# Projecting the first chunks before the attention jobs, or between them

## The chip, the cores and the metric

The kernel runs on one core of a Trainium2 chip. The metric is the device time of one execution in microseconds (us), the median of several runs. Times inside an execution are read from a profile of one such execution and count from its first instruction.

## What is computed

Two transformer layers on `x` of 4 sequences x 1024 rows x 128 columns, in fp32. Each layer adds attention (16 heads of 8 columns) and then a gated feed-forward net, each on the layer-normalised `x`. The attention of the first layer sees all keys, that of the second is causal. The core of the reference:

```python
def attention(x, Wqkv, bqkv, Wout, bout):
    qkv = (x @ Wqkv + bqkv).reshape(b, s, H, 3 * HD)
    q, k, v = qkv[..., :HD], qkv[..., HD:2 * HD], qkv[..., 2 * HD:]
    scores = jnp.einsum('bqhd,bkhd->bhqk', q, k) / jnp.sqrt(HD)
    out = jnp.einsum('bhqk,bkhd->bqhd', jax.nn.softmax(scores), v)
    return out.reshape(b, s, e) @ Wout + bout

x = x + attention_a(layernorm(x));  x = x + ffn(layernorm(x))
x = x + attention_b(layernorm(x));  x = x + ffn(layernorm(x))
```

The weights of the net are integers that are scaled by 1/127 first.

## The kernel before, in words

**Tiling.** The 4096 rows are 8 chunks of 512 (`CHUNKS`), two to a sequence. For each chunk VectorE computes the row statistics (`row_moments`), POOL raises the variance to the power -0.5 (`inverse_deviation`), VectorE normalises four tiles (`normalise`, line 706), TensorE transposes them (`transpose_tiles`, line 938), ScalarE copies the result (`copy_xt`), and TensorE makes the products (`qkv_products`: q and k at line 948, v at line 950). ScalarE takes q and k with their bias and rounds them (`take_qk`, lines 528 and 532); VectorE adds the bias to v and writes it into the tile `v`, and then subtracts the rounded q and k from the exact ones (`split_chunk`, lines 725 and 729), so that a q or k is held as two parts. The SyncE queue (SP) writes the parts to DRAM (`store_parts`).

**Windows.** Attention runs over 16 windows: one sequence and 4 of its heads each. SP loads the queries and keys of a window from DRAM into one of three buffers of `qop` and `kop` (`load_operands`, 14 DMAs). Rows of `qop` and `kop` that no load writes must be filled once with zeros and ones. TensorE's *jobs* (line 995) compute scores for their row maxima alone, 64 for a window in layer one, and VectorE reduces each to a maximum (`run_job`, line 785, or 782 on the diagonal). Jobs use a ring of three PSUM banks. When a half of a window (512 queries) has its 32 jobs, VectorE negates the maxima (`negate_max`), POOL splits them (`split_shift`), TensorE transposes them, ScalarE copies them to `shift_rows`, and SP writes them by two DMAs into the last rows of `qop` (`shift_to_operand`, line 373). Only then can TensorE compute the shifted *scores* of that half (line 1009), whose exponential ScalarE takes (line 559) and which TensorE multiplies with v (line 1045).

**Order.** The engines each run a hand-made list. `Plan` makes it. `plan.before` is what comes ahead of the steady part in each layer: in layer one 54 jobs, with the shift of the first half after job 35 and scores from job 42 on. The *turns* follow, one for each window: the scores of window w between the rest of its jobs and the first jobs of window w + 1. Between the two layers there is a `middle` part, in which the feed-forward net of layer one runs and the chunks are projected for layer two.

**Start of layer one before.** VectorE runs the moments and the normalising of chunks 0 and 1, statistics of chunks 2 to 7 at once, then all eight chunks in one pipeline (`first_chunk` on each engine), then the scaling of the integer weights (line 767). POOL fills `v` with ones between the power of chunk 0 and that of chunk 1 (line 437), and the rows of all three `kop` buffers after the latter (line 444). ScalarE fills the rows of all three `qop` buffers first (line 510). SP's queue in order: stores of chunks 0 to 3, loads of window 0, stores of chunks 4 to 7, loads of window 1, the first shift. TensorE starts with jobs when `qk_ready` and `v_ready` say that all eight chunks are taken; after jobs 4, 8 and 12 it transposes a third of the scaled weights (line 971).

## Time and profile before

| what | us |
|---|---|
| median of 3 runs | 1576.52 |
| lowest and highest | 1567.07, 1581.94 |
| the profiled execution's own time | 1573.21 |
| its span, first to last instruction | 1571.4 |
| TensorE, VectorE, ScalarE busy in it | 1438.6, 1235.9, 980.0 |

### The profile page before, as it was taken

How to read it: one execution, taken by the hardware profiler on the slowest of the kernel's cores; microseconds unless marked ns; L12 is line 12 of the kernel's file. 1: busy time of each engine (PE TensorE's matmuls, PEld its weight loads, DVE VectorE, ACT ScalarE, POOL GpSimd, SP SyncE). 2: the span in 40 equal slices, each digit the busy share in tenths (PEclk: the TensorE clock that was granted, in tenths of full speed). 3: DMA queues.
4: the chain of work that ended last, by engine and by line, in shares of the span. 5: the costliest groups of instructions: out<-in, count | busy, mean ns of one | idle time of the engine just before them, and what ended most of it. 6: DMA issues, size and time to landing. Idle time of an engine off the chain costs nothing.

```text
span 1571.4 us, 26128 instructions
## 1 busy us (share of the span) xinstructions
PE 1438.6 (92%) x9625; PEld 701.7 (45%) x9625; DVE 1235.9 (79%) x3106; ACT 980.0 (62%) x1259; POOL 108.9 (7%) x210
## 2 busy tenths in 40 slices
PE   3699999999999999999988988999999999999888
PEld 2444344434444443444436654444444444444455
DVE  7589999999999998999937757787787877777254
ACT  4427777777777777777774432666666666666622
POOL 6020000000000000000001112000000000000010
PEclk9859999999999999999999985999999999999999
DMA  3720111111101111110001323111121112210000
GB/s 95 221 57 7 27 28 29 29 29 28 28 6 25 28 28 29 28 28 2 2 1 54 83 79 76 35 29 29 29 53 32 29 29 47 38 29 2 8 21 27
DMA packets 40055, 58.39 MB, mean 37 GB/s; under 512 B 7796, under 2 KB 19448, under 8 KB 39928
## 3 DMA queue, kind: packets, MB, share of 16 engines
q1 hardware_dynamic: 39928, 56.72, 15.2%
q8 instruction: 76, 1.25, 0.3%
q14 instruction: 51, 0.42, 0.1%
HBM read 36.77 MB, written 18.87 MB: 35 GB/s over the span
## 4 chain that ended last, share of the span: by engine, by line
PE 70%; DVE 18%; ACT 5%; issue 4%; DMA 2%; SPq 1%; POOL 0%; DVEq 0%; ACTq 0%; POOLq 0%
PE psum L995 25%; PE psum L1045 23%; DVE maxima L785 11%; PE psum L1009 6%; PE psum L1142 5%; PE psum L938 4%; ACT probs L559 3%; DVE junk L782 3%; PE psum L1147 2%; PE psum L1017 1%; PE psum L948 1%; DVE xn L706 1%; PE psum L1062 1%; DMA k_parts<-parts 1%; DMA qop<-shift_rows 1%
## 5 line engine op out<-in xcount | busy, mean ns | idle before, releaser
L559 ACT ACTIVATE probs<-psum 128x1024 f32<-128x1024 f32 (+3 forms) x896 | 794.2, 932 | 300.4 <-PE psum L1009 192.7
L785 DVE TENSOR_REDUCE maxima<-psum 128x1 f32<-128x512 f32 x1280 | 815.2, 684 | 72.8 <-PE psum L995 67.8
L995 PE MATMUL psum<-kop,qop 62*128 62x512 f32 (+3 forms) x1792 | 657.0, 465 | 56.5 <-DVE maxima L782 20.0
L1009 PE MATMUL psum<-qop,kop 64*128 64x512 f32 (+3 forms) x1792 | 498.2, 411 | 10.4 <-ACT probs L559 7.8
L995 PEld LDWEIGHTS psum<-kop,qop 62*128 62x128 f32 x1792 | 289.6, 191 | 487.6 <-DVE maxima L785 325.4
L1045 PE MATMUL psum<-probs,vwin 128*32 128x512 f32 (+3 forms) x3584 | 441.6, 565 | 3.9 <-ACT probs L559 2.0
L782 DVE CUSTOM_DVE_ANT_0 junk<-psum,mask 128x384 bf16<-128x384 f32 (+3 forms) x512 | 237.4, 487 | 75.3 <-PE psum L995 69.8
L1009 PEld LDWEIGHTS psum<-qop,kop 64*128 64x128 f32 x1792 | 242.0, 189 | 55.7 <-ACT probs L559 44.7
L1045 PEld LDWEIGHTS psum<-probs,vwin 128*32 128x32 f32 x3584 | 71.8, 109 | 105.5 <-issue 84.6
L1017 PE MATMUL psum<-half_ident,key_mask 64*128 64x64 bf16 x1024 | 92.7, 198 | 0.0
L1142 PE MATMUL psum<-ffn_xt,wffn 128*128 128x512 f32 x192 | 87.6, 594 | 0.0
L463 POOL TENSOR_TENSOR shift<-negmax,zeros 128x16 bf16<-128x16 f32 x64 | 14.1, 220 | 1017.5 <-DVE negmax L791 1017.5
L796 DVE RECIPROCAL rden<-att_raw 128x16 f32<-128x16 f32 x64 | 15.8, 247 | 61.3 <-ACT att_raw L580 61.3
L656 ACT ACTIVATE hid<-psum 128x512 f32<-128x512 f32 x48 | 28.7, 597 | 52.0 <-PE psum L1142 52.0
L1147 PE MATMUL psum<-wffn,hid 128*128 128x128 f32 x384 | 48.7, 278 | 7.9 <-DVE hid L899 7.9
L1017 PEld LDWEIGHTS psum<-half_ident,key_mask 64*128 64x128 bf16 x1024 | 49.7, 97 | 13.1 <-issue 1.3
L899 DVE TENSOR_TENSOR hid<-psum,hid 128x512 f32<-128x512 f32 x48 | 32.4, 689 | 26.8 <-PE psum L1142 21.4
L1147 PEld LDWEIGHTS psum<-wffn,hid 128*128 128x128 f32 x384 | 45.2, 192 | 15.4 <-DVE hid L899 15.4
L575 ACT CAST shift_rows<-psum 32x128 f32<-32x128 bf16 x64 | 16.3, 254 | 56.7 <-PE psum L1027 56.7
L714 DVE TENSOR_TENSOR x<-psum,x 128x512 f32<-128x512 f32 x32 | 22.1, 690 | 37.4 <-PE psum L1147 29.1
L1142 PEld LDWEIGHTS psum<-ffn_xt,wffn 128*128 128x128 f32 x192 | 34.2, 191 | 31.9 <-issue 31.0
L938 PEld LDWEIGHTS psum<-ident,sums 128*128 128x128 f32 x256 | 26.8, 140 | 44.9 <-ACT probs L559 40.2
(88 smaller groups left out, 709.9 us busy)
## 6 DMA issues: line engine op xcount, KB each, us to landing
qop<-q_parts SPq DMA_DIRECT2D x256, 64.0 KB
q_parts<-parts SPq DMA_DIRECT2D x32, 256.0 KB, 3.0
k_parts<-parts SPq DMA_DIRECT2D x32, 256.0 KB, 3.4
kop<-k_parts SPq DMA_DIRECT2D x64, 128.0 KB
kop<-k_parts SPq DMA_DIRECT2D x128, 64.0 KB
x<-in_L_attn_a_x SPq DMA_DIRECT2D x8, 256.0 KB, 4.4
qop<-shift_rows SPq DMA_DIRECT2D x128, 8.0 KB
out_x<-x SPq DMA_DIRECT2D x8, 256.0 KB, 2.3
```

The lines of the kernel that those rows point to most:

```text
L559: nc.scalar.activation(probs[:, slot, :, c0:], psum[:, bank:bank + 2, c0:], ACT.Exp, scale=SCORE_SCALE).then_inc(probs_ready, 1)
L656: nc.scalar.activation(hid[:, c, :], psum[:, 2 + 2 * (c % 2), :], ACT.Silu).then_inc(silu_ready, 1)
L782: nc.vector.tensor_tensor_reduce(out=junk[:, slot, 0:width], in0=src, in1=mask[:, CHUNK - width:], scale=1.0, scalar=LOWEST, op0=ALU.add, ...
L785: nc.vector.tensor_reduce(dst, src, AX_X, ALU.max).then_inc(ring_free, 1)
L899: nc.vector.tensor_tensor(hid[:, c, :], psum[:, 3 + 2 * (c % 2), :], hid[:, c, :], ALU.mult).then_inc(hid_ready, 1)
L938: ins = nc.tensor.transpose(psum[:, bank, t * P:(t + 1) * P], src[:, t, :], ident[:])
L995: mm(psum[:, slot, 0:width], qop[rows, buf, f, r, qb * P:(qb + 1) * P].bitcast(F32R), kop[rows, buf, r, kh * CHUNK:kh * CHUNK + width].bit ...
L1009: ins = mm(psum[:, bank + h, c0:], kop[rows, buf, pair, j * P:(j + 1) * P].bitcast(F32R), qop[rows, buf, f, pair, c0:].bitcast(F32R), star ...
L1017: ins = mm(psum[:, bank + h, at:at + TILE_ROWS], key_mask[rows, part, :], half_ident[rows], start=False, stop=part == 1)
L1045: ins = mm(psum[32 * c:32 * c + 32, 7, c0:], vwin[:, buf, at:at + 32], probs[:, slot, c % 2, c0:], start=(j == 0), stop=(s == plan.half_en ...
L1142: mm(psum[:, 2 + 2 * (c % 2) + k, :], wffn[:, k, c, :], ffn_xt[:], start=True, stop=True).then_inc(gate_up_psum, 1)
L1147: ins = mm(psum[:, 7, t * P:(t + 1) * P], hid[:, c, t * P:(t + 1) * P], wffn[:, 2, c, :], start=(c == 0), stop=(c == FB - 1))
```

## The change

- The list of layer one gets new events: before jobs 4, 9, 14, 19, 24 and 29 a chunk (2 to 7), before job 34 the weights. Ahead of the jobs only chunks 0 and 1, the first sequence, are projected. At event n each engine does: VectorE normalises chunk n + 1 and splits chunk n - 1; TensorE transposes chunk n + 1 and multiplies chunk n; ScalarE copies and takes them. In the jobs' part v has one PSUM bank and q and k have two, since the ring takes the others. The weights event also splits chunk 7.
- SP stores chunks 0 and 1, then loads window 0, then stores chunks 2 to 7, then loads window 1. `load_operands` waits itself for the stores of its sequence alone. It takes the keys and first queries first and counts the four DMAs of the second half's queries on another semaphore. Each chunk of `x` has a semaphore of its own, and the weights of layer two are loaded after `x`.
- POOL fills a quarter of `v` with its first constants, the rest after chunk 1 is normalised, and the `kop` rows of buffers 1 and 2 after the last chunk is normalised. ScalarE fills the rows of `qop` and `kop` for buffer 0 first, those of `qop` buffers 1 and 2 in the chunk events 2 and 3.
- The statistics of chunks 2 to 7 come in three pieces while VectorE would wait. The biases of layer two are spread after the products of chunk 1.

The core of the diff (blank lines left out):

```diff
+        chunk_at = {4 + chunk_jobs * i: ("chunk", 2 + i) for i in range(CHUNKS - 2)} if chunk_jobs else {}
+        weights_at = 4 + chunk_jobs * (CHUNKS - 2)
...
+            if k in chunk_at:
+                events.append(chunk_at[k])
+            if chunk_jobs and k == weights_at:
+                events.append(("weights",))
...
-    LOADS = 2 * 7 * SEM_DMA
+    LOADS = 2 * 5 * SEM_DMA
+    LATE_LOADS = 2 * 2 * SEM_DMA
...
             load_x(0, x_loaded[0])
-            for l, (w, b, bo) in enumerate(((wqkv_a, bqkv_a, bout_a), (wqkv_b, bqkv_b, bout_b))):
-                sp.dma_start(wqkv_raw[:, l, :], w).then_inc(qkv_weights_loaded, SEM_DMA)
-                sp.dma_start(bias_raw[0:1, l, :], b.rearrange("(o n) -> o n", o=1)).then_inc(qkv_weights_loaded, SEM_DMA)
-                sp.dma_start(bias_row[0:1, l, 3, :], bo.rearrange("(o n) -> o n", o=1)).then_inc(qkv_weights_loaded, SEM_DMA)
-            load_x(1, x_loaded[1])
-            for c in range(2, CHUNKS):
-                load_x(c, x_loaded[2])
+            load_qkv_weights(0, wqkv_a, bqkv_a, bout_a)
+            for c in range(1, CHUNKS):
+                load_x(c, x_loaded[c])
+            load_qkv_weights(1, wqkv_b, bqkv_b, bout_b)
...
-            def load_operands(w, buf):
+            def load_operands(layer, w, buf):
                 q_heads = q_parts[bass.ds(w, 1)].rearrange("o (r i) d t -> i d (o r) t", i=2)
                 k_heads = k_parts[bass.ds(w, 1)].rearrange("o (r i) d t -> i d (o r) t", i=2)
+                def load_queries(i, f, loaded):
+                    for row in (TILE_ROWS * i, TILE_ROWS * i + PD):
+                        sp.dma_start(qop[row:row + PD, buf, f], q_heads[i, :, :, f * CHUNK:(f + 1) * CHUNK]).then_inc(loaded, SEM_DMA)
+                for p in range(2):
+                    sp.wait_ge(parts_stored[p], (layer * B + w // GROUPS + 1) * STORES)
                 for i in range(2):
                     base = TILE_ROWS * i
-                    for f in range(2):
-                        for row in (base, base + PD):
-                            sp.dma_start(qop[row:row + PD, buf, f],
-                                         q_heads[i, :, :, f * CHUNK:(f + 1) * CHUNK]).then_inc(operands_loaded[buf], SEM_DMA)
+                    load_queries(i, 0, operands_loaded[buf])
                     for row, part in ((base, slice(0, PD)), (base + PD, slice(HD, PD)), (base + PD + HD, slice(0, HD))):
                         sp.dma_start(kop[row:row + part.stop - part.start, buf], k_heads[i, part]).then_inc(operands_loaded[buf], SEM_DMA)
+                for i in range(2):
+                    load_queries(i, 1, late_operands_loaded[buf])
             for layer, plan in enumerate(PLANS):
-                for i in range(B // 2):
+                for half in range(2):
+                    store_parts(layer, 0, half)
+                if layer == 0:
+                    load_operands(layer, 0, 0)
+                for i in range(1, B):
                     for half in range(2):
                         store_parts(layer, i, half)
-                for p in range(2):
-                    sp.wait_ge(parts_stored[p], (layer * B + B // 2) * STORES)
-                if layer == 0:
-                    sp.wait_ge(ones_ready, 2)
-                    sp.wait_ge(operands_zeroed, 2)
-                load_operands(0, 0)
-                for i in range(B // 2, B):
-                    for half in range(2):
-                        store_parts(layer, i, half)
-                for p in range(2):
-                    sp.wait_ge(parts_stored[p], (layer + 1) * B * STORES)
-                load_operands(1, 1)
+                    if layer == 1 and i == 1:
+                        load_operands(layer, 0, 0)
+                load_operands(layer, 1, 1)
...
+            nc.gpsimd.memset(v[:, 0:GROUPS * VW], 1.0).then_inc(v_set, 1)
...
-            nc.gpsimd.memset(v[:], 1.0).then_inc(v_set, 1)
             inverse_deviation(2, first_moments[:, :, TPC:2 * TPC], 2)
-            pool.wait_ge(rstd_ready[2], 2)
-            for i in range(2):
-                row = TILE_ROWS * i + GUARD_ROW
-                nc.gpsimd.memset(kop[row:row + SCORE_ROWS - GUARD_ROW], 1.0).then_inc(ones_ready, 1)
-                pool.wait_ge(ones_ready, i + 1)
+            pool.wait_ge(xn_ready[0], 2)
+            nc.gpsimd.memset(v[:, GROUPS * VW:], 1.0).then_inc(v_set, 1)
             inverse_deviation(2, first_moments[:, :, 2 * TPC:], 3)
             for layer, plan in enumerate(PLANS):
-                pool.wait_ge(v_ready, (layer + 1) * CHUNKS)
                 sums_base = layer * WINDOWS * PLANS[0].n
                 half_base = layer * 2 * WINDOWS
                 def copy_v(w, buf):
+                    chunks = min(2 * (w // GROUPS) + 2 + (w % GROUPS == GROUPS - 1), CHUNKS)
+                    pool.wait_ge(v_ready, layer * CHUNKS + chunks)
...
+                if layer == 0:
+                    pool.wait_ge(vwin_ready, 2)
+                    pool.wait_ge(xn_ready[0], CHUNKS)
+                    for u in range(1, BUFS):
+                        for i in range(2):
+                            row = TILE_ROWS * i + GUARD_ROW
+                            nc.gpsimd.memset(kop[row:row + SCORE_ROWS - GUARD_ROW, u], 1.0).then_inc(ones_ready, 1)
+                            pool.wait_ge(ones_ready, 2 * u + i - 1)
...
-            for i in range(2):
-                rows = slice(TILE_ROWS * i + GUARD_ROW, TILE_ROWS * i + SCORE_ROWS)
-                nc.scalar.copy(qop[rows].rearrange("p u f r t -> p (u f r t)").bitcast(F32R),
-                               zeros[rows, 0:1].broadcast_to([SCORE_ROWS - GUARD_ROW, BUFS * PAIRS * S])).then_inc(operands_zeroed, 1)
...
+            def fill_rows(tile, u, source):
+                for i in range(2):
+                    rows = slice(TILE_ROWS * i + GUARD_ROW, TILE_ROWS * i + SCORE_ROWS)
+                    dst = tile[rows, u].bitcast(F32R)
+                    nc.scalar.copy(dst, source[rows].broadcast_to([SCORE_ROWS - GUARD_ROW, PAIRS * S])).then_inc(operands_zeroed, 1)
+            qop_rows = qop[:].rearrange("p u f r t -> p u (f r t)")
+            kop_rows = kop[:].rearrange("p u r t -> p u (r t)")
+            fill_rows(qop_rows, 0, zeros[:, 0:1])
+            fill_rows(kop_rows, 0, one[:])
+            def take_biases(l, qk_bank, vo_bank, column):
+                act.wait_ge(setup_psum, l + 1)
+                nc.scalar.copy(bqk[:, l, :], psum[:, qk_bank, 0:2])
+                nc.scalar.copy(bvo[:, l].rearrange("p t e -> p (t e)"), psum[:, vo_bank, column:column + 2 * E]).then_inc(setup_ready, 1)
+            take_biases(0, 6, 7, 0)
...
+            copy_xt(1, 1, 1)
+            take_qk(0, 0, 0, 2)
+            take_qk(0, 1, 1, 5)
+            take_biases(1, 0, 0, 2 * E)
+            copy_xt(2, 0, 0)
+            def chunk(n):
+                if n + 1 < CHUNKS:
+                    copy_xt(n + 1, (n + 1) % 2, (n + 1) % 2)
+                take_qk(0, n, n % 2, 2)
+                if 2 <= n < BUFS + 1:
+                    fill_rows(qop_rows, n - 1, zeros[:, 0:1])
...
+                    if kind == "chunk":
+                        chunk(what[0])
+                    elif kind == "weights":
+                        for k in range(3):
+                            act.wait_ge(setup_psum, 3 + k)
+                            nc.scalar.copy(wffn[:, k].rearrange("p c d -> p (c d)"), psum[:, k, 0:HIDDEN]).then_inc(setup_ready, 1)
...
-            dve.wait_ge(x_loaded[0], SEM_DMA)
-            first_row_moments(0, 1, 0)
-            dve.wait_ge(qkv_weights_loaded, 6 * SEM_DMA)
+                moments_of(2, first_stats[:, tiles], first_moments[:, :, tiles], count)
+            def first_normalise(n):
+                normalise(0, n, first_moments, n * TPC, xn[:, n % 2], n - 1)
+            first_row_stats(0, 1).then_inc(moment_steps[2], 1)
+            first_moments_of(0, 1, 0)
+            dve.wait_ge(qkv_weights_loaded[0], 3 * SEM_DMA)
             order_columns(0)
             dve.wait_ge(rstd_ready[2], 1)
-            normalise(0, 0, first_moments, 0, xn[:, 0], 0)
-            order_columns(1)
-            dve.wait_ge(x_loaded[1], SEM_DMA)
-            first_row_moments(1, 1, 1)
+            first_normalise(0)
+            first_row_stats(1, 1).then_inc(moment_steps[2], 1)
+            first_moments_of(1, 1, 1)
+            first_row_stats(2, 2)
             dve.wait_ge(rstd_ready[2], 2)
-            normalise(0, 1, first_moments, TPC, xn[:, 1], 0)
-            dve.wait_ge(x_loaded[2], (CHUNKS - 2) * SEM_DMA)
-            first_row_moments(2, CHUNKS - 2, 2)
-            dve.wait_ge(rstd_ready[2], 3)
+            first_normalise(1)
+            first_row_stats(4, 2)
             dve.wait_ge(setup_ready, 1)
             dve.wait_ge(v_set, 1)
-            def first_chunk(n, buf, m):
-                if m + 2 < CHUNKS:
-                    normalise(0, n + 2, first_moments, (n + 2) * TPC, xn[:, buf], n + 1)
-                split_chunk(0, n, buf, 4 + 3 * buf)
-            pipeline(dve, first_chunk)
-            dve.wait_ge(other_weights_loaded, 5 * SEM_DMA)
-            nc.vector.tensor_scalar(wflt, wint, DEQUANT, None, ALU.mult).then_inc(wflt_ready, 1)
+            split_chunk(0, 0, 0, 4)
+            first_row_stats(6, 2).then_inc(moment_steps[2], 1)
+            first_moments_of(2, CHUNKS - 2, 2)
+            split_chunk(0, 1, 1, 7)
+            dve.wait_ge(qkv_weights_loaded[1], 3 * SEM_DMA)
+            order_columns(1)
+            dve.wait_ge(rstd_ready[2], 3)
+            first_normalise(2)
+            dve.wait_ge(v_set, 2)
+            def chunk(n):
+                if n + 1 < CHUNKS:
+                    first_normalise(n + 1)
+                if n > 2:
+                    split_chunk(0, n - 1, (n - 1) % 2, 7)
...
+                    elif kind == "weights":
+                        chunk(CHUNKS)
+                        dve.wait_ge(other_weights_loaded, 5 * SEM_DMA)
+                        nc.vector.tensor_scalar(wflt, wint, DEQUANT, None, ALU.mult).then_inc(wflt_ready, 1)
...
+            transpose_xn(1, 1, 1)
             pe.wait_ge(setup_ready, 1)
-            pipeline(pe, first_chunk)
+            qkv_products(0, 0, 0, 2, 4)
+            qkv_products(0, 1, 1, 5, 7)
+            spread_biases(1, 0, 0, 2 * E)
+            pe.wait_ge(setup_ready, 2)
+            transpose_xn(2, 0, 0)
+            def chunk(n):
+                if n + 1 < CHUNKS:
+                    pe.wait_ge(xt_ready[0], n)
+                    transpose_xn(n + 1, (n + 1) % 2, (n + 1) % 2)
+                pe.wait_ge(qk_ready, 2 * n)
+                pe.wait_ge(v_ready, n)
+                qkv_products(0, n, n % 2, 2, 7)
...
+                        if layer == 0 and lap == 0:
+                            pe.wait_ge(operands_zeroed, 4 + 2 * buf)
+                            wait(pe, ones_ready, 2 * buf)
+                    if (f, c, qb, kh) == (1, 0, 0, 0):
+                        earlier = layer * len(range(buf, WINDOWS, BUFS))
+                        pe.wait_ge(late_operands_loaded[buf], (lap + earlier + 1) * LATE_LOADS)
...
-                        if layer == 0 and index in (4, 8, 12):
-                            pe.wait_ge(wflt_ready, 1)
-                            transpose_weights(index // 4 - 1)
+                        continue
+                    if kind == "chunk":
+                        chunk(what[0])
+                        continue
+                    if kind == "weights":
+                        pe.wait_ge(wflt_ready, 1)
+                        pe.wait_ge(xt_ready[0], CHUNKS)
+                        pe.wait_ge(qk_ready, 2 * CHUNKS)
+                        for k in range(3):
+                            transpose_weights(k)
                         continue
                     if layer == 0 and unit == 0:
-                        pe.wait_ge(setup_ready, 4)
+                        pe.wait_ge(setup_ready, 5)
+                        pe.wait_ge(v_ready, CHUNKS)
```

## Rows read from the trace of the kernel before

**Rows 1.** The page: the chain that ended last, share of the span by engine.
```profile
PE 70%; DVE 18%; ACT 5%; issue 4%; DMA 2%; SPq 1%; POOL 0%; DVEq 0%; ACTq 0%; POOLq 0%
```

**Rows 2.** Timeline to 36 us: start, duration (us), engine, line, operation, tiles, shapes, count, [idle before].
```profile
6.49 3.96 POOL L437 MEMSET v<- 128x4631 f32 x1
6.57 4.53 DVE L706 TENSOR_SCALAR xn<-x,first_moments 128x128 f32<-128x128 f32 x4 [0.23 <-POOL first_moments L434]
...
14.81 10.69 DVE L706 TENSOR_SCALAR xn<-x,first_moments 128x128 f32<-128x128 f32 x4 [1.13 <-POOL first_moments L434]
14.83 10.51 POOL L444 MEMSET kop<- 32x6144 f32 x2
...
25.42 4.72 DVE L687 BATCH_NORM_STATS2 first_stats<-x 128x6 f32<-128x128 f32 x24
...
31.34 4.16 POOL L434 TENSOR_TENSOR first_moments<-first_moments,power 128x24 f32<-128x24 f32 x1 [5.99 <-DVE first_moments L700]
```

**Rows 3.** The same timeline: chunks in the projection stretch, at both clock levels.
```profile
26.52 3.11 PE L948 MATMUL psum<-xt,wqkv 128*128 128x512 f32 x4
...
29.47 1.05 PE L950 MATMUL psum<-wqkv,xt 128*128 128x128 f32 x8
...
35.53 1.12 DVE L706 TENSOR_SCALAR xn<-x,first_moments 128x128 f32<-128x128 f32 x4 [4.35 <-POOL first_moments L434]
36.57 0.88 DVE L725 TENSOR_TENSOR v<-psum,bvo 128x128 f32<-128x128 f32 x4
...
36.80 1.09 PE L938 MATMUL psum<-ident,xn 128*128 128x128 f32 x4 [6.28 <-DVE xn L706]
...
37.68 3.62 PE L948 MATMUL psum<-xt,wqkv 128*128 128x512 f32 x4
...
41.09 1.80 PE L950 MATMUL psum<-wqkv,xt 128*128 128x128 f32 x8
...
43.16 1.88 PE L948 MATMUL psum<-xt,wqkv 128*128 128x512 f32 x4
```

**Rows 4.** The same timeline: the first jobs, the weights, the first scores.
```profile
73.41 1.19 PE L995 MATMUL psum<-kop,qop 62*128 62x512 f32 x3 [11.63 <-DVE v L725]
...
75.20 0.75 DVE L767 TENSOR_SCALAR probs<-probs 128x1152 f32<-128x1152 int32 x1
...
80.44 0.90 PE L971 MATMUL psum<-ident,probs 128*128 128x128 f32 x3
...
85.24 12.65 DVE L785 TENSOR_REDUCE maxima<-psum 128x1 f32<-128x512 f32 x21 [0.65 <-PE psum L995]
...
102.28 1.21 PE L1009 MATMUL psum<-qop,kop 64*128 64x512 f32 x2
```

**Rows 5.** Windows: busy us (instructions) per engine, granted clock, DMA share, GB/s.
```profile
90.00:100.00 10.00, 10.00 (x19) 4.83 (x18) 10.00 (x19) 0.26 (x1) 1.86 (x3) 0.50 0.00 1
...
1106.00:1110.00 4.00, 4.00 (x43) 2.11 (x38) 3.48 (x18) 2.15 (x3) 0.00 (x0) 0.70 0.44 118
```

**Rows 6.** Two source lines: the subtraction from 70 to 80 us, POOL's copy; durations ns min/median/max.
```profile
L729 DVE TENSOR_TENSOR parts<-qk,parts x2: 1226/1350/1475, 71.3 to 73.8; 128x1024 f32<-128x1024 f32 x2
...
L454 POOL COPY vwin<-v x32: 439/443/1370, 73.4 to 1391.7; 128x311 f32<-128x311 f32 x32
```

**Rows 7.** The chain in order of time, start of layer two: start, duration (us), what.
```profile
945.66 3.01 DMA k_parts<-parts
...
955.29 4.84 DMA qop<-shift_rows
```

**Rows 8.** Timeline of SP's queue: window 1's loads and the first shift.
```profile
80.30 1.71 SPq L342 DMA_DIRECT2D qop<-q_parts  x4
82.07 1.12 SPq L345 DMA_DIRECT2D kop<-k_parts  x3
...
99.30 1.41 SPq L373 DMA_DIRECT2D qop<-shift_rows  x2
```

**Rows 9.** Timeline of TensorE, first scores of layer two.
```profile
960.18 0.80 PE L1009 MATMUL psum<-qop,kop 64*128 64x512 f32 x2 [0.42 <-DMA qop<-shift_rows]
```

More of the change, by code:

```diff
@@ L135, in __init__ @@
         self.last_ends = [[x for x in self.turn_ends[i] if x[0] == 0] for i in own]
-        self.units_before = sum(kind != "job" for kind, *_ in self.before)
+        self.units_before = sum(kind in ("shift", "exp") for kind, *_ in self.before)
         self.units_turn = 2 * n + sum(map(len, self.turn_ends))
@@ L377, in _ @@
                         shift_to_operand(what[0], 0, unit)
-                    if kind != "job":
+                    if kind in ("shift", "exp"):
                         unit += 1
@@ L641, in _ @@
                         exp_unit(0, 0, what[0], what[1], unit, unit)
-                    if kind != "job":
+                    if kind in ("shift", "exp"):
                         unit += 1
```

79 lines of the change are left out of this document (39 added, 40 removed).

## The prediction

> **What bounds the kernel now.** I read the chain that ended last first: TensorE carries 70% of the span and VectorE 18% [rows 1]. The body, some 1,460 us, is out of the change's reach: its jobs, exponentials and sums stay, and each window still issues 14 loads. So the question is what the stretch before the first scores is worth. The timeline shows it in three pieces [rows 2].
>
> First, the fills. The four instructions that normalise chunk 0 take 4.53 us beside a 3.96 us fill of `v`, and those of chunk 1 take 10.69 us beside a 10.51 us fill of `kop`; later the same four take 1.12 us [rows 2, 3]. 3.4 + 9.6 = 13.0 us of VectorE is waiting. Second, all eight chunks are projected before TensorE's first job, at 73.41 us, and it waited 11.63 us for VectorE's last `v`, which stood behind stores and loads [rows 4]. Third, from there VectorE alone sets the pace: 21 maxima in 12.65 us, 0.60 us each [rows 4]. The first scores start at 102.28 us [rows 4], so 28.9 us after the first job. TensorE's granted clock is 0.50 there, the 1.2 GHz level, although its row shows no idle [rows 5].
>
> **The new start, step by step.** Up to 6.4 us nothing changes. POOL now fills a quarter of `v` first (3.96 / 4 = 1.0 us), which moves its first power to an end near 7.0 us. Normalising chunk 0: 1.12, to 8.1. Statistics of chunk 1 (24 take 4.72 us, so 0.2 each [rows 2]) 0.9, moments about 0.9, to 9.9; the power ends at 10.9 and VectorE's eight statistics at 11.5; normalise chunk 1 to 12.6. Transposes 1.09 to 13.8. ScalarE's first fills write two thirds of what they wrote before, when they were not late either; they end before the transposes do, and nobody waits. The products of chunk 0 take 3.62 + 1.80, overlapped 5.2 us, at the low clock throughout, or 4.0 (26.52 to 30.5) where it rises on the way [rows 3]; I take 4.4, to 18.2. VectorE: `v` 0.88 and the subtraction 1.22 to 20.4; statistics 1.6 and moments 1.1 to 23.1; `v` and subtraction of chunk 1 to 25.2.
>
> Here lies a new collision: the 24-column power (4.16 us [rows 2]) starts at 23.1 on POOL, the subtraction at 24.0. The trace has no such pair. Its nearest rows are the same subtraction beside POOL's copy of `v`: once it took 1.475 instead of 1.22 us, and once the copy took 1.37 instead of 0.44 [rows 6]. So one of them held up the other. Bounds: 0, and held to the power's end, 3.3 us. The slowed subtraction lost 0.25 us where some 0.4 us were shared, so I take 60%, 2.0 us: to 27.2. The Trainium skill (SBUF — State Buffer, section "SBUF: two separate sides") says that a VectorE instruction with two SBUF inputs and a GpSimd instruction that reads SBUF exclude each other for the whole instruction; the two rows agree in kind. By that rule the term is the full 3.3 us and the forecast 1.3 us later. It also says that GpSimd's pure fills don't hold such a subtraction, which speaks for costing the moved `kop` fills at nothing.
>
> Stores: the second is issued near 27.8 and lands after 3.01 us (the row of the second layer [rows 7]): 30.8. SP then issues ten loads, 4 x 0.43 + 6 x 0.375 = 4.0 us from the 1.71 and 1.12 us groups [rows 8]; the last starts at 34.5. Its landing is not shown. Bounds: 1 us, and 4.84 us, of a transfer that followed 14 loads [rows 7]; I take 3.0, the store's. First job: 37.5 us, that is 35.9 us earlier.
>
> **What the interleaving costs.** After job 3 and then after every five jobs, each engine meets a chunk. VectorE does it in order: it can normalise chunk n+1 only behind its last maximum, then adds the `v` of chunk n-1; TensorE waits for the normalised tiles, and its products of chunk n wait for that `v` (one bank now); the next jobs stand behind the products in TensorE's queue. Nothing of this overlaps maxima. One cycle:
> - five maxima, 3.1
> - normalise 1.12, then `v` 0.85 beside the transposes: 2.06 at the high clock, 2.35 at the low one (1.12 + 0.15 + 1.09)
> - products: 2.8 (1.88 + 1.05, overlapped) to 5.2
> - first job to its maximum: 0.5 to 0.8
> The sum is 8.5 at the high clock throughout, 11.5 at the low one, and 10.0 with the 4.0 us products. The subtraction (1.22) hides under the products. Which clock? It rose twice while products ran (the later matmuls of rows 3 take half the time of the earlier), it stayed at 0.50 through the jobs, and in one stretch of the body it fell to 0.70 though TensorE's row is full [rows 5]. I take 10.0: it falls in the job part of a cycle and rises again in the products. Five such cycles: 50.0. The first chunk has no `v` to add: 1.12 + 0.15 + 1.09 + 4.0 + 0.5 = 6.9.
>
> The weights event: `v` 0.85, subtraction 1.22, scaling 0.75 (rows 3, 6 and 4), then nine transposes at 0.30 us (0.90 for three [rows 4]) or half of that. Job 34 would follow after 4.6 to 6.1 us, and the first scores some 3.8 us later: 8.4 to 9.9 us after the event begins. But they also need the shift rows, and SP reaches those last: the stores of chunk 7 wait for that event's subtraction (2.1 us), take 1.2 to issue, then come the 14 loads of window 1 (5.9 us), then two shift issues 0.7 apart (1.41 for both [rows 8]), whose landing took 4.84 us behind the same loads in layer two [rows 7]. 2.1 + 1.2 + 5.9 + 0.7 + 4.84 = 14.8 us. Before, window 1's loads were issued at 80.30 and the shift followed at 99.30 with an empty queue: so the landing lies between 2.3 (from 100.0 to the scores at 102.28 [rows 4, 8]) and 4.84. I take 4.84, since the loads stand directly in front. So the wait for operands is replaced by one for the shift, some 5 us long, with TensorE's remaining jobs queued behind it and VectorE drained.
>
> From first job to first scores: 0.8 + 2.4 (jobs 0 to 3) + 6.9 + 50.0 + 3.1 (jobs 29 to 33) + 14.8 = 78.0 us, before 28.9. **Sum:** 49.1 - 35.9 = 13.2 us later at the first scores. Behind them the same work follows.
>
> The rest: in layer two load_operands(1) no longer waits for the last stores, so the shift leaves earlier; the idle that its transfer ended there was 0.42 us [rows 9], so -0.4. The four `kop` fills (10.51 / 6 = 1.75 us each) run from the last normalisation on, beside a subtraction that has at least 1.6 us of cover; if they blocked it entirely, 7 us, some 3 us would show. I take 0. The late queries' semaphore is met long before the second half's jobs: 0. POOL's waits for `v` per window: 0; its copies still stand ready before the sums. Total +12.8 us. The profiled execution took 1573.2 us, 3.3 us under the runs' median of 1576.5; against its own time that gives 1586.0.
>
> **The rivals.**
> 1. *The high clock holds through the interleaved part.* For it: the chunk stretch of before, once risen, kept it [rows 3]. Against: in the job stretch it stays at 0.50 [rows 5]. Price: cycles 8.5 in place of 10.0, -7.5; no products at the low clock in the first chunk, -1.2; the first turn started with the low clock, some 2 us. That is -10.7, and with no hold by the power (-2.0) and a landing of 2 us in place of 3 (-1) the time is 1572: not slower. It decides from a cycle of 7.4 us downward alone (13.2 / 5 = 2.6 less), or 8.5 with the others.
> 2. *The low clock throughout.* The rows of the job stretch speak for it, the two rises in the first 42 us against it. Cycles of 11.5 add 7.5, the first chunk 1.5: 1595.
> 3. *A hold on VectorE that isn't gone but moved*: power in full (+1.3) and the `kop` fills onto the subtraction (+3): 1590.
> 4. *The change doesn't start the jobs early*: the ten loads land at the upper bound and the stores are congested; the landing 1.8 later and the stores 2 later, the first job near 41.5, 1590.
>
> **How the numbers follow.** Forecast 0.50 (own range 1580 to 1592), rival 1 0.19, rival 2 0.19, rivals 3 and 4 0.06 each. The range 1573 to 1598 leaves out about 2 in 10: rival 1's better half and rival 2's upper tail. Within 1% of the median (1560.8 to 1592.3), about what can be told from no change, lie the forecast, rival 1, and most of 3 and 4: 0.75. Slower by over 1%: rival 2 and the forecast's edge, 0.21. Faster by over 1% needs 12 us that no term has: 0.04.
>
> **What would show it.** Four normalising instructions near 1.1 us for chunks 0 and 1; the first job at 36 to 40 us; the maxima in groups of five with 9 to 11 us between their starts; the granted clock up and down between 0.50 and 1.00 from 40 to 100 us; an idle of TensorE ended by the shift rows' transfer before the first scores, near 115 us. The prediction is wrong if the cycle is under 8 us, if the first scores start before 104 us, or if the body's turns change.

## The result, and the profile after

The kernel after takes 1596.93 us, the median of 4 runs (1591.62 to 1602.41); the kernel before, in 4 runs beside it, 1575.61 us. The ratio is 1.0146, with a 95% interval of 1.0110 to 1.0182: slower by 21.3 us, 1.46%. The forecast was 1586.0 us, 0.6% over the median it knew, in a range of 1573 to 1598; being slower by over 1%, which is what came, had a chance of 0.21, staying within 1% one of 0.75. The profiled execution took 1599.9 us, its span is 1598.1 us, 26.7 us over the span before.

The page of the profile of the kernel after: the granted clock in 40 slices, and the chain that ended last.

```profile
PEclk7667999999999999999999995899999999999999
...
PE 70%; DVE 19%; ACT 4%; issue 4%; DMA 1%; SPq 1%; POOL 0%; DVEq 0%; POOLq 0%; ACTq 0%
```

Against [rows 1] the shares hardly move: a change at the start alone can't be seen in an average over 1,600 us. The place has to be found in the timeline. The start first, all engines (start, duration, engine, line, operation, count, and in brackets the idle time before and what ended it):

```profile
6.88 1.11 DVE L746 TENSOR_SCALAR xn<-x,first_moments 128x128 f32<-128x128 f32 x4 [0.27 <-POOL first_moments L445]
...
11.13 1.10 DVE L746 TENSOR_SCALAR xn<-x,first_moments 128x128 f32<-128x128 f32 x4
...
12.29 3.00 POOL L450 MEMSET v<- 128x3479 f32 x1 [1.54 <-DVE xn L746]
...
22.76 4.16 POOL L445 TENSOR_TENSOR first_moments<-first_moments,power 128x24 f32<-128x24 f32 x1 [7.48 <-DVE first_moments L740]
23.39 1.22 DVE L769 TENSOR_TENSOR parts<-qk,parts 128x1024 f32<-128x1024 f32 x1
...
28.28 0.82 SPq L351 DMA_DIRECT2D qop<-q_parts  x2
...
31.13 1.13 SPq L359 DMA_DIRECT2D kop<-k_parts  x3
32.30 1.70 SPq L351 DMA_DIRECT2D qop<-q_parts  x4
...
37.82 1.22 PE L1066 MATMUL psum<-kop,qop 62*128 62x512 f32 x3 [8.30 <-DMA kop<-k_parts]
```

The eight normalising instructions of chunks 0 and 1 take 2.2 us, where [rows 2] have 15.2. The first job starts at 37.82 us where [rows 4] have 73.41: 35.6 us earlier, as forecast.

Then one chunk between five jobs, from 59 to 69 us:

```profile
59.21 3.08 DVE L837 TENSOR_REDUCE maxima<-psum 128x1 f32<-128x512 f32 x5 [4.40 <-PE psum L1066]
...
62.21 1.11 DVE L746 TENSOR_SCALAR xn<-x,first_moments 128x128 f32<-128x128 f32 x4
63.23 0.88 DVE L765 TENSOR_TENSOR v<-psum,bvo 128x128 f32<-128x128 f32 x4
...
63.47 1.08 PE L998 MATMUL psum<-ident,xn 128*128 128x128 f32 x4 [2.42 <-DVE xn L746]
64.03 1.22 DVE L769 TENSOR_TENSOR parts<-qk,parts 128x1024 f32<-128x1024 f32 x1
...
64.34 3.62 PE L1008 MATMUL psum<-xt,wqkv 128*128 128x512 f32 x4
...
67.76 1.33 PE L1010 MATMUL psum<-wqkv,xt 128*128 128x128 f32 x8
```

VectorE and TensorE take turns: normalise, transpose, products, the next job, and no maximum runs beside them. The fives of maxima start at 48.78, 59.21, 69.56, 79.86, 90.13 and 99.85 us, so a cycle takes 10.43 us at first and 9.72 for chunk 7, which has nothing left to normalise. The windows of the same stretch (busy time by engine, granted clock, DMA):

```profile
58.70:61.20 2.50, 1.71 (x6) 0.65 (x5) 1.99 (x4) 2.48 (x2) 0.00 (x0) 1.00 0.24 49
61.20:64.40 3.20, 0.93 (x5) 0.93 (x6) 3.20 (x11) 1.96 (x2) 0.00 (x0) 0.55 0.36 125
64.40:67.80 3.40, 3.40 (x6) 1.32 (x6) 0.84 (x1) 1.27 (x2) 0.00 (x0) 0.50 0.38 107
67.80:69.10 1.30, 1.30 (x11) 1.18 (x9) 0.00 (x0) 1.06 (x2) 0.00 (x0) 0.79 0.35 123
...
60.60:61.60 1.00, 0.45 (x1) 0.14 (x1) 1.00 (x2) 0.98 (x2) 0.00 (x0) 0.96 0.94 248
```

The clock does alternate between its two levels, but later in the cycle than forecast: it is 1.00 in the jobs, where VectorE sets the pace and it is of no use, and 0.50 in the transposes and most of the products, where TensorE sets it. TensorE's last job of the five ended at 61.05 us, and the clock fell just before 61.6, inside TensorE's wait of 2.42 us for the normalised tiles; it rose again at the end of the products, near 68.3. So transposes and products took 5.5 us (63.47 to 69.02).

Last, the weights event, which costs most against the forecast:

```profile
102.94 0.88 DVE L765 TENSOR_TENSOR v<-psum,bvo 128x128 f32<-128x128 f32 x4
103.04 8.80 POOL L489 TENSOR_TENSOR x<-x,bvo 128x4096 f32<-128x4096 f32 x1
103.73 9.20 DVE L769 TENSOR_TENSOR parts<-qk,parts 128x1024 f32<-128x1024 f32 x1
112.84 0.75 DVE L923 TENSOR_SCALAR probs<-probs 128x1152 f32<-128x1152 int32 x1
...
113.65 2.18 PE L1035 MATMUL psum<-ident,probs 128*128 128x128 f32 x9 [11.96 <-DVE probs L923]
114.21 1.02 SPq L351 DMA_DIRECT2D qop<-q_parts  x2
...
120.57 1.41 SPq L382 DMA_DIRECT2D qop<-shift_rows  x2
...
125.50 0.80 PE L1080 MATMUL psum<-qop,kop 64*128 64x512 f32 x2 [4.21 <-DMA qop<-shift_rows]
```

The subtraction of chunk 7 takes 9.20 us, and the same instruction took 1.22 in every chunk before it. POOL's addition of the output bias to the whole of `x` runs from 103.04 to 111.84. Behind the subtraction stand the scaling, TensorE's transposes, the last stores, the 14 loads of window 1 and then the shift. The chain of waits of this stretch has both pieces on it:

```profile
103.81 9.12 DVE parts L769
...
121.35 4.11 DMA qop<-shift_rows
```

The first scores start at 125.50 us, 23.2 later than before; window 2's copy of `v` on POOL at 133.68, 22.8 later. From there the body is the same: window 15's copy is at 692.7 before and at 715.6 after (+23.0), the last one of layer two at 1391.7 and 1415.0 (+23.2). Layer two has windows of 31.75 us, and single ones that take up to 5.5 us more, at other places in each trace; in one such stretch of before the clock is at 0.90:

```profile
1103.70:1138.00 34.30, 32.31 (x268) 16.92 (x269) 25.21 (x86) 20.75 (x31) 1.40 (x6) 0.90 0.15 33
```

and near the end of after, where before has 1.00 throughout, at 0.96:

```profile
1503.20:1533.20 30.00, 27.16 (x125) 16.61 (x123) 15.76 (x54) 10.62 (x17) 2.60 (x3) 0.96 0.06 18
```

Such a fall fits the 3.5 us between +23.2 at that copy and +26.7 for the span. Over the ten traces the time from the first scores to the end grows, on the whole, with the part of it that the clock spends at 0.50: 1466.2 us with 61 us of it in b1 (the shortest), 1469.1 with 67 in before, 1472.6 with 73 in after, 1477.3 with 89 in d1 (the longest). What gives one execution more of it than another, no run tests. So the experiments are read at the first scores, and the medians are the check on them.

### The profile page after: what moved, and what is told of

Same layout as the page of the kernel before. It is cut to its first block, busy times and chain, and to the rows that moved or that the text cites. A ratio compares the mean times of both kernels' runs of the same rounds, so it can differ in the third digit from the quotient of the medians.

```text
span 1598.1 us, 26232 instructions
## 1 busy us (share of the span) xinstructions
PE 1448.1 (91%) x9625; PEld 706.5 (44%) x9625; DVE 1231.2 (77%) x3106; ACT 985.5 (62%) x1267; POOL 104.7 (7%) x214
## 4 chain that ended last, share of the span: by engine, by line
PE 70%; DVE 19%; ACT 4%; issue 4%; DMA 1%; SPq 1%; POOL 0%; DVEq 0%; POOLq 0%; ACTq 0%
PE psum L1066 24%; PE psum L1116 23%; DVE maxima L837 12%; PE psum L1080 6%; PE psum L1221 5%; PE psum L998 4%; ACT probs L589 3%; DVE junk L834 3%; PE psum L1008 3%; PE psum L1226 2%; PE psum L1088 1%; PE psum L1010 1%; PE psum L1133 1%; DVE parts L769 1%; DVE xn L746 1%
## 5 line engine op out<-in xcount | busy, mean ns | idle before, releaser
L1080 PE MATMUL psum<-qop,kop 64*128 64x512 f32 (+3 forms) x1792 | 498.6, 412 | 13.6 <-ACT probs L589 7.7
L1066 PEld LDWEIGHTS psum<-kop,qop 62*128 62x128 f32 x1792 | 286.4, 190 | 482.1 <-DVE maxima L837 323.5
L469 POOL TENSOR_TENSOR shift<-negmax,zeros 128x16 bf16<-128x16 f32 x64 | 14.1, 220 | 1014.5 <-DVE negmax L843 1014.5
L848 DVE RECIPROCAL rden<-att_raw 128x16 f32<-128x16 f32 x64 | 15.9, 248 | 61.6 <-ACT att_raw L610 61.6
L1088 PEld LDWEIGHTS psum<-half_ident,key_mask 64*128 64x128 bf16 x1024 | 49.8, 97 | 12.8 <-issue 1.2
L1008 PE MATMUL psum<-xt,wqkv 128*128 128x512 f32 x64 | 44.8, 839 | 8.2 <-ACT xt L545 5.3
```

The lines of the kernel that those rows point to most:

```text
L1008: mm(psum[:, qk_banks + t, :], wqkv[:, layer, t, :], xt[:, buf, :], start=True, stop=True).then_inc(qkv_psum, 1)
L1066: mm(psum[:, slot, 0:width], qop[rows, buf, f, r, qb * P:(qb + 1) * P].bitcast(F32R), kop[rows, buf, r, kh * CHUNK:kh * CHUNK + width].bit ...
L1080: ins = mm(psum[:, bank + h, c0:], kop[rows, buf, pair, j * P:(j + 1) * P].bitcast(F32R), qop[rows, buf, f, pair, c0:].bitcast(F32R), star ...
L1088: ins = mm(psum[:, bank + h, at:at + TILE_ROWS], key_mask[rows, part, :], half_ident[rows], start=False, stop=part == 1)
```

## The experiments

Each is timed beside the kernel before on the same chip. Medians of before: 1573.25 us for a1 to c1, 1575.38 for the last four. Before has its first job at 73.41 us and its first scores at 102.28.

| run | median us | ratio to before | first job | first scores |
|---|---|---|---|---|
| after | 1596.93 | 1.0146 [1.0110, 1.0182] | 37.82 | 125.50 |
| a1_bias_late | 1589.23 | 1.0110 [1.0089, 1.0132] | 38.04 | 114.77 |
| a2_loads_early | 1594.85 | 1.0136 [1.0116, 1.0155] | 37.87 | 117.88 |
| a3_both | 1586.91 | 1.0082 [1.0062, 1.0103] | 37.49 | 112.63 |
| c1_chunks_ahead | 1566.99 | 0.9961 [0.9948, 0.9974] | 61.36 | 91.91 |
| d1_spare_work | 1581.42 | 1.0032 [1.0017, 1.0047] | 36.82 | 103.45 |
| b1_fills_only | 1557.29 | 0.9899 [0.9880, 0.9918] | 59.72 | 88.65 |
| b2_fills_loads | 1554.91 | 0.9881 [0.9861, 0.9900] | 57.32 | 84.61 |
| c2_chunks_ahead | 1567.79 | 0.9947 [0.9931, 0.9963] | 54.11 | 91.22 |

The medians don't follow the first scores exactly. In the six experiments on the changed kernel (a, c and d) the median lies 3.3 to 6.0 us further up against before than the first scores do; in b1 and b2 it lies 4.5 and 2.8 us further down. The extra time at the low clock behind the first scores is of that size in most of the traces, but there is one trace for each, so this part stays open.

### The bias addition later (a1)

```diff
                 pool.wait_ge(xn_ready[0], (layer + 1) * CHUNKS)
+                pool.wait_ge(part2_ready, (layer + 1) * CHUNKS)
+                pool.wait_ge(wflt_ready, 1)
                 nc.gpsimd.tensor_tensor(x[:], x[:], bvo[:, layer, 1:2, :].broadcast_to([P, TILES, E]), ALU.add).then_inc(x_biased, 1)
```

> The changed kernel, with POOL's addition of the output bias to x held back until the last subtraction and the scaled weights are done. Theory H (the 8.80 us addition reads SBUF and holds VectorE's subtraction, 9.20 us in place of 1.22, with stores, window 1's loads and the shift behind it): the subtraction back to 1.22 us, first scores 8 us earlier (117.5 in place of 125.5), the time 8 us under the changed kernel's. Rival R (the subtraction was slow for its own reason, the parts' stores or PSUM): still about 9 us, time unchanged. In the addition's new place VectorE only reads PSUM, so nothing should be held there.

The timeline of a1:

```profile
101.42 1.22 DVE L771 TENSOR_TENSOR parts<-qk,parts 128x1024 f32<-128x1024 f32 x1
...
103.48 8.85 POOL L491 TENSOR_TENSOR x<-x,bvo 128x4096 f32<-128x4096 f32 x1 [2.71 <-DVE probs L925]
...
114.77 0.80 PE L1082 MATMUL psum<-qop,kop 64*128 64x512 f32 x2 [3.77 <-DMA qop<-shift_rows]
```

The subtraction is back at 1.22 us, the addition takes its 8.85 us beside maxima that don't mind it, and from the addition of `v` to the first scores it is 14.1 us (100.63 to 114.77) instead of 22.6: 8.4 us won there. The median is 16.0 us over its own before, where after has 21.3: 5.3 us less, where 8 were expected. The intervals overlap, so the price is taken from the trace. That the hold is gone with its neighbour is shown.

One more difference is in the trace: a1 reaches the addition of `v` 2.3 us sooner than after. Its cycles begin at 9.8 and 10.0 us, with a granted clock of 0.83 in the windows from 48 to 78 us where after has 0.66 to 0.67. a2's do the same, a3's don't (10.3 to 10.6). a1's edit acts at 100 us for the first time and can't do that; which phase the clock falls into differs from execution to execution, worth 2.3 us here and 2.6 in a2.

### Window 1's loads ahead of the stores (a2), and both (a3)

```diff
                 if layer == 0:
                     load_operands(layer, 0, 0)
+                    load_operands(layer, 1, 1)
...
-                load_operands(layer, 1, 1)
+                if layer == 1:
+                    load_operands(layer, 1, 1)
```

> The changed kernel, with window 1's 14 loads issued right behind window 0's instead of behind chunk 7's stores. Theory S (the shift rows' transfer stands behind these loads; it ended a wait of 4.21 us): the shift's issue comes as soon as ScalarE's copy is there (117.5 us), first scores near 120.5, 5 us earlier, time 4 to 5 us under the changed kernel's. Rival (the wait is the transfer's own latency or the late copy): under 1 us.

> Both edits together. If the hold and the loads are two separate delays in a row, 12 to 13 us under the changed kernel: first scores near 112.5 us and the time 8 to 10 us over the kernel before. If they hide one another, no more than the larger one, 8 us. What is then left over the kernel before is the interleaving itself.

The queue and TensorE in a2:

```profile
101.11 9.19 DVE L771 TENSOR_TENSOR parts<-qk,parts 128x1024 f32<-128x1024 f32 x1
...
114.89 1.41 SPq L384 DMA_DIRECT2D qop<-shift_rows  x2
...
117.88 1.21 PE L1082 MATMUL psum<-qop,kop 64*128 64x512 f32 x2
```

and in a3:

```profile
103.84 1.22 DVE L773 TENSOR_TENSOR parts<-qk,parts 128x1024 f32<-128x1024 f32 x1
...
109.64 1.42 SPq L384 DMA_DIRECT2D qop<-shift_rows  x2
...
112.63 1.21 PE L1084 MATMUL psum<-qop,kop 64*128 64x512 f32 x2
```

With nothing in front of it the shift's transfer is covered by the jobs, and the scores have no wait. From the addition of `v` to the first scores a2 takes 17.6 us (5.0 less than after), a3 9.6 (13.0 less, near 8.4 + 5.0). So the two delays stood in a row. a2's median shows nothing of its 5 us: it is 21.6 us over its before, where after has 21.3 and 4 to 5 less were expected; after's interval is some 11 us wide, so the price of the loads rests on the traces, and on a3's median, which is 2.3 us under a1's. In a3 the first scores still stand 10.3 us behind those of before (112.63 against 102.28), where the moved fills alone would put them 13.6 ahead (b1, below). The median is 13.7 us over before, where 8 to 10 were expected.

### All chunks ahead of the jobs (c1)

a3, and the six chunk events ahead of job 0 instead of between the jobs; the rest as in a3.

```diff
-        chunk_at = {4 + chunk_jobs * i: ("chunk", 2 + i) for i in range(CHUNKS - 2)} if chunk_jobs else {}
+        if chunk_jobs:
+            events += [("chunk", 2 + i) for i in range(CHUNKS - 2)]
...
-            if k in chunk_at:
-                events.append(chunk_at[k])
```

> The changed kernel with both edits of a3_both and all six chunk events in front of job 0, the weights still before job 34. Nothing else changes. Theory I (interleaving costs because each chunk serialises VectorE, TensorE and the jobs, with the low clock half of the time): chunk cycles of about 4 us without jobs, first job near 57 us, first scores near 88, the time 20 to 25 us under a3_both's and 11 to 15 under the kernel before. Rival (the cost is the later weights event and the single bank for v, both kept here): within 5 us of a3_both.

TensorE in c1:

```profile
41.39 1.98 PE L1011 MATMUL psum<-xt,wqkv 128*128 128x512 f32 x4 [2.39 <-ACT qk L556]
...
48.20 3.78 PE L1011 MATMUL psum<-xt,wqkv 128*128 128x512 f32 x4 [2.73 <-ACT qk L556]
...
61.36 0.73 PE L1069 MATMUL psum<-kop,qop 62*128 62x512 f32 x3
```

The median is 19.9 us under that of a3, just short of the 20 to 25 that were expected, with the same instructions in another order. The rival, within 5 us of a3, is out. Its first job comes 23.9 us later than a3's, and its first scores 20.7 us sooner: from there VectorE makes 33 maxima in 19.82 us without a break. Against before the gain is 6.3 us where 11 to 15 were expected. About 4 us of that is the late start (first scores at 91.91 where 88 were expected): ScalarE's fills of `qop` lie between the chunks, 3.82 us each at 35.62 and 42.44 us, and with two banks TensorE has to wait for ScalarE (2.39 and 2.73 us).

### The fills alone (b1), and the loads with them (b2)

b1 is the kernel before with nothing but the fills moved, as the change moves them. Its core:

```diff
+            nc.gpsimd.memset(v[:, 0:GROUPS * VW], 1.0).then_inc(v_set, 1)
...
-            nc.gpsimd.memset(v[:], 1.0).then_inc(v_set, 1)
...
-            pool.wait_ge(rstd_ready[2], 2)
-            for i in range(2):
-                row = TILE_ROWS * i + GUARD_ROW
-                nc.gpsimd.memset(kop[row:row + SCORE_ROWS - GUARD_ROW], 1.0).then_inc(ones_ready, 1)
-                pool.wait_ge(ones_ready, i + 1)
+            pool.wait_ge(xn_ready[0], 2)
+            nc.gpsimd.memset(v[:, GROUPS * VW:], 1.0).then_inc(v_set, 1)
...
+                if layer == 0:
+                    pool.wait_ge(wflt_ready, 1)
...
+                            nc.gpsimd.memset(kop[row:row + SCORE_ROWS - GUARD_ROW, u], 1.0).then_inc(ones_ready, 1)
...
+            fill_rows(qop_rows, 0, zeros[:, 0:1])
+            fill_rows(kop_rows, 0, one[:])
```

> The kernel before with its order of chunks and jobs, only the fills moved off the normalisations (a quarter of v first, the rest after chunk 1; the rows of buffer 0 by ScalarE first; the other buffers after the weights). Theory: the 13 us that VectorE lost beside the fills were on the path to the first job, so it comes 12 us earlier (61.4 in place of 73.4) and the time is 11 to 13 us under the kernel before. Rival: the stores and window 0's loads, which held the projection for 10 us from 60 us on, eat it, and the gain is half of that or less.

The timeline of b1:

```profile
6.82 1.11 DVE L718 TENSOR_SCALAR xn<-x,first_moments 128x128 f32<-128x128 f32 x4 [0.30 <-POOL first_moments L436]
...
11.64 1.11 DVE L718 TENSOR_SCALAR xn<-x,first_moments 128x128 f32<-128x128 f32 x4 [1.13 <-POOL first_moments L436]
...
59.72 1.19 PE L1010 MATMUL psum<-kop,qop 62*128 62x512 f32 x3 [11.77 <-DVE v L737]
...
88.65 1.22 PE L1024 MATMUL psum<-qop,kop 64*128 64x512 f32 x2
```

The first job is 13.7 us earlier than before, the first scores 13.6, the median 18.1 us lower (0.8 to 1.2%), where 11 to 13 were expected. Where the 4.5 us between the two come from isn't settled; they are of the size of the spread. The 13.0 us that the prediction read off two fills are all there. The wait for the last `v`, 11.63 us before [rows 4], stays at 11.77.

b2 adds the changed `load_operands` and puts window 0's loads ahead of the last chunk's stores instead of behind chunk 3's:

```diff
+            for i in range(B):
+                if layer == 0 and i == B - 1:
+                    sp.wait_ge(operands_zeroed, 4)
+                    load_operands(layer, 0, 0)
                 for half in range(2):
                     store_parts(layer, i, half)
```

> b1_fills_only with the changed kernel's load_operands (waits for its own sequence, ten loads first) and window 0's loads between the stores of chunks 5 and 6 in place of behind the stores of chunk 3. Theory: the projection's 10 us stall goes too, since no store that ScalarE waits for stands behind the loads; the first job near 55.5 us, 18 us earlier than before, and the time 16 to 19 us under the kernel before. Rival: the loads now land last and TensorE waits for them, first job at 60 or later, no gain over b1_fills_only.

TensorE in b2:

```profile
57.32 1.19 PE L1012 MATMUL psum<-kop,qop 62*128 62x512 f32 x3 [8.65 <-DMA kop<-k_parts]
...
84.61 1.21 PE L1026 MATMUL psum<-qop,kop 64*128 64x512 f32 x2
```

The first job comes at 57.32, 2.4 earlier than in b1 and 1.8 later than expected: the wait is no longer for `v` but for the loads, which now land last, as the rival had it. Its time is 20.5 us under before, where 16 to 19 were expected. The first scores are 4.0 us ahead of b1's, the medians only 2.4 apart, and the intervals of b1 and b2 overlap. b1 against b2 stays open; both beat the kernel before, and every version with jobs ahead of chunks.

### c1 with a shorter way to the first job (c2)

ScalarE's two fills go from the chunks to the weights event, and window 1's loads from behind window 0's to between the last stores.

```diff
                 take_qk(0, n, n % 2, 2)
-                if 2 <= n < BUFS + 1:
-                    fill_rows(qop_rows, n - 1, zeros[:, 0:1])
...
                             nc.scalar.copy(wffn[:, k].rearrange("p c d -> p (c d)"), psum[:, k, 0:HIDDEN]).then_inc(setup_ready, 1)
+                        for u in range(1, BUFS):
+                            fill_rows(qop_rows, u, zeros[:, 0:1])
```

> c1_chunks_ahead with ScalarE's fills of qop buffers 1 and 2 in the weights event and window 1's loads between the stores of chunks 6 and 7. In c1 TensorE waited 2.39 and 2.73 us for q and k behind ScalarE's fills and 1.6 us for a store. Theory: these 6 us go, first job near 55.5 us in place of 61.4, time 5 us under c1's. Rival (another engine's order takes over the same waits): under 2 us.

ScalarE in c2:

```profile
80.53 7.65 ACT L531 CAST qop<-zeros 32x2048 fp32r<-32x2048 f32 x4
88.21 0.26 ACT L607 CAST shift_rows<-psum 32x128 f32<-32x128 bf16 x1
```

and TensorE:

```profile
91.22 0.79 PE L1084 MATMUL psum<-qop,kop 64*128 64x512 f32 x2 [5.77 <-DMA qop<-shift_rows]
```

A miss with a lesson. The first job comes at 54.11 us, 7.3 earlier than in c1, but the first scores only 0.7. The median is 7.6 us under before, c1's 6.3, with overlapping intervals: the 5 us that were expected can't be seen, and at the first scores the rival (under 2 us) is right. The fills now stand in front of the copy of the shift rows in ScalarE's list. TensorE has the transposed rows at 81.4 us, the copy starts at 88.21; so the shift lands late, and TensorE waits 5.77 us. The 7.65 us were moved from one short path to another. The two shift issues begin at 88.49 us on an empty queue, and the transfer lands some 2.0 us after the second; in the kernel after, behind the 14 loads, it was 4.2.

### Spare transposes to keep the clock up (d1)

a3, with a transpose behind each of jobs 4 to 33 and eight ahead of those of each chunk. Nobody reads what they write; this run asks only what the clock is worth.

```diff
+            def spare(bank, count):
+                for _ in range(count):
+                    nc.tensor.transpose(psum[:, bank, 0:P], ident[:], ident[:])
...
                     pe.wait_ge(xt_ready[0], n)
+                    spare((n + 1) % 2, 8)
                     transpose_xn(n + 1, (n + 1) % 2, (n + 1) % 2)
...
+                        if layer == 0 and 4 < index <= 34:
+                            spare(last_chunk % 2, 1)
```

> a3_both with spare transposes that nobody reads on TensorE: one behind each of jobs 4 to 33 and eight ahead of each chunk's transposes, where TensorE waits for VectorE. Theory C (part of each interleaved cycle is the low clock): the granted clock stays at 1.00 from 50 to 100 us and the cycles shrink from 10.3 to 8.5 or 8.8 us, so 7 to 8 us less over the five, time 5 to 8 us under a3_both's. Rival (the cycle is the serial chain through VectorE, whatever the clock; or the spare work delays the chunk's transposes): cycles stay above 10, time equal or longer.

The window from 58 to 68 us of d1:

```profile
58.00:68.00 10.00, 8.45 (x38) 4.99 (x38) 7.72 (x22) 3.45 (x5) 0.00 (x0) 1.00 0.35 105
```

and of a3:

```profile
58.00:68.00 10.00, 6.93 (x21) 3.68 (x20) 6.03 (x14) 6.24 (x6) 0.00 (x0) 0.67 0.33 96
```

The clock holds at 1.00 for four cycles, which take 8.65 to 8.67 us each (fives of maxima at 45.49, 54.16, 62.81, 71.47 and 80.14). In a3 they take 10.3 to 10.6. In the fifth the clock falls after all, at 83 us, and that cycle takes 10.4. So the low clock is at least 1.7 us of a cycle. The first scores come 9.2 us earlier (112.63 to 103.45), of which 0.7 stand at the first job already. Against its own before d1 is 7.6 us better than a3 (6.0 over it in place of 13.7), in the 5 to 8 that were expected. The other 8.66 us are the serial way through two engines: the five maxima of a cycle are worth 3.1 us (3.4 in d1, with the spare work between), and the rest buys one chunk. Ahead of the jobs, in c1, the six chunks cost 61.4 - 37.5 = 23.9 us, 4.0 each, with ScalarE's fills among them. d1 is still slower than before, by 0.3%.

## Why the prediction was right or wrong

The measured time lies inside the stated range, but at its upper end, which was meant for rival 2, the low clock throughout, and that didn't come: the range held it by luck. The way from the first job to the first scores, by the prediction's own steps (us):

| step | forecast | after |
|---|---|---|
| first job | 37.5 | 37.8 |
| jobs 0 to 3 | 3.2 | 3.3 |
| first chunk | 6.9 | 7.7 |
| five cycles | 50.0 | 51.1 |
| jobs 29 to 33 | 3.1 | 3.1 |
| weights event to first scores | 14.8 | 22.6 |
| first scores | 115.5 | 125.5 |

- **The fills**: right. 13.0 us were read off; b1 has 13.7 at the first job.
- **The first job**: right in sum, by luck, since two errors cancel. The power was to hold up the subtraction for 2.0 us; it held it for none (1.22 us beside a power of 4.16). So the loads start at 28.28 us and not at 30.8. But the last of the ten, issued by 32.26, is awaited until 37.82: some 5.6 us or more, where 3.0 were taken and 4.84 was the upper bound. Four further loads stand directly behind it; 14 more behind those (a2, a3) left the first job at 37.87 and 37.49.
- **The cycle**: right in size (10.0 and 10.2 on average) and in its chain of waits. The products took 4.7 us (64.34 to 69.02) where 4.0 were taken, since the clock fell later than the forecast had it and rose only at their end; the fifth cycle was shorter (9.72), since chunk 7's event has nothing left to normalise, which the forecast overlooked. Rival 1, the high clock throughout, did not come by itself; d1 shows what it would have been, 8.66 where 8.5 were worked out. Rival 2, low throughout, didn't come either: the windows have 0.67, not 0.50. What the clock does between the two varies from execution to execution (a1).
- **The weights event**: here is the step that failed. The term took the subtraction of chunk 7 at 1.22 us ("`v` 0.85, subtraction 1.22, scaling 0.75"), and the part "The rest" looked at POOL's `kop` fills and copies of `v` as its neighbours but not at the bias addition, which waits only for the last normalisation and for the list ahead of it. It costs 8.0 us (9.20 - 1.22), and a1 takes 8.4 back. The row was there to see: in the trace before the same addition starts at 98.53 us, beside maxima, and lasts 8.87.

```profile
98.53 8.87 POOL L474 TENSOR_TENSOR x<-x,bvo 128x4096 f32<-128x4096 f32 x1
```

What moved was not the addition but the subtraction, into its time. That was a rival nobody priced: rival 3 had the right kind of hold (moved, not gone) with the wrong culprits, the power and the fills. The `kop` fills left their subtraction at 1.22 us, as the prediction had it. The forecast also read the two pairs of [rows 6] as a partial hold, 60% of what was shared. They fit a full one: the slowed copy shared 1.07 us with the subtraction, lost 0.93 and ended 0.30 after it; the slowed subtraction ended 1.08 us after the copy.
- **The shift behind window 1's loads**: right. The wait is 4.21 us, the step had some 5, and a2 takes 5.0 us back by moving the loads.
- **The body**: right that its turns stay. -0.4 us for layer two is below what the clock's single falls, up to 5.5 us each, let one see.
- **The base**: the +12.8 us were set on an execution that was 3.3 us under the median, so that the forecast stood 9.5 us over the median and not 12.8.

With the hold priced at its 8.0 us the sum would have been +20.8, that is 1594.0 us against the profiled execution's 1573.2, and the difference measured between medians is 21.3. The subtraction, whose tiles all lie in SBUF (the memory of all tiles here but `psum`), starts 0.69 us after the addition and ends 1.09 us after the addition's end, which is nearly its own 1.22 us: it is held to the end. The Trainium skill (SBUF — State Buffer, section "SBUF: two separate sides") says so of a VectorE instruction with two SBUF inputs beside a GpSimd instruction that reads SBUF. The prediction weighed that rule for the power, where the trace now contradicts it, and didn't apply it to the addition, where the trace agrees.

So the change holds a gain and two losses, by the first scores: the fills alone bring them to 88.65 us (b1, before 102.28), with the chunks between the jobs they come 24.0 later than that (a3, 112.63), of which 20.7 are the placing alone (a3 against c1), and the held subtraction with the late shift the other 12.9 (after, 125.50).

## What to carry to other kernels

Before work is slotted between other work, ask what overlaps in each place. Here the chunks ran as a pipeline over three engines at 4.0 us each, and slotted between jobs each ran through two engines in turn, so that a cycle of 10.3 us, five maxima worth 3.1 us among it, bought one chunk; starting the jobs 36 us earlier didn't pay for six of these. And whenever an instruction is moved later, list what the other engines do at its *new* time, above all the long instructions that no queue ties to it: an 8.8 us addition with no hurry at all cost 8.0 us through one subtraction. Moving the fills off the normalisation alone is worth 1.0%, and was the part to keep.

## What the runs showed that was not expected

- VectorE's subtraction of two SBUF tiles is held to the end of POOL's addition of two SBUF tiles, for all of the 8 us, where the slowed pairs of [rows 6], on short copies, had lost only 0.25 and 0.93 us: 9.20 and 9.19 us beside it (after, a2), 1.22 us away from it (a1, a3).
- POOL's power of 24 columns, whose inputs lie in SBUF too, doesn't do that: the subtraction began 0.63 us after it and took 1.22 us, and the power took 4.16, as it does alone [rows 2].
- A normalising instruction (SBUF in, SBUF out, one tile of input) is held by a POOL fill, by 3.4 and 9.6 us for the four of a chunk in the kernel before, and by nothing in b1, where the fills are moved away; the subtraction isn't: 1.22 us at 84.67 us, while POOL's fill ran from 84.09.
- The clock's phase against the cycle differed between executions, at 0.67 (after, a3) or 0.83 (a1, a2) on average. Spare transposes between the waits kept it at 1.00, and made each cycle 1.7 us shorter, although the engine had more to do.
